# Attention and a mixture of experts on one core: transposes and similarities ahead of down products, one-hots by VectorE only

## The reference

```python
def xattn(h, adj_raw, Wq, Wk, gamma_raw):      # h = ctx, adj_raw = layernorm(x)
    Q = (h @ Wq.T) in 4 heads; K = (h @ Wk.T) in 4 heads
    sim = einsum('bhnd,bhmd->bnm', Q, K) / (sqrt(32) * 4)
    threshold = top_k(sim, 153)[..., -1:]       # a row's 153rd largest
    A = sigmoid(sim) * (sim >= threshold)
    A = (A + swapaxes(A, -1, -2)) * 0.5
    return (1 - gamma) * adj_raw + gamma * A    # gamma = sigmoid(gamma_raw)
x = x + xattn(ctx, layernorm(x), ...)
h = layernorm(x)                                # 2048 rows
scores = sigmoid(h @ router_w)                  # 32 experts in 8 groups of 4
# biased scores: best 4 groups (by their top 2), of them the best 8 experts of a row
w = scores of the 8 / their sum * 2.5
routed = sum over the 8 of w * (silu(h @ w_gate[e]) * (h @ w_up[e])) @ w_down[e]   # inner size 256
shared = (silu(h @ sw_gate) * (h @ sw_up)) @ sw_down                               # inner size 512
x = x + routed + shared
```

## Time and profile before

| what | us |
|---|---|
| median of three runs (1103.67 to 1105.88) | 1104.59 |
| the profiled execution, whole time | 1106.17 |
| its span, from first to last instruction | 1104.4 |
| stage 0, up to the bound of stage 1 | 93.5 |
| stages 1, 2 | 77.9, 78.3 |
| stage 3, to the end of the first block | 72.5 |
| from there to the expert tiles at full pace (375) | 52.8 |
| expert tiles | 729 |
| TensorE, VectorE, ScalarE, POOL busy | 921.8, 573.0, 487.4, 481.6 |

### The profile page before, as it was taken

The page is one execution under the profiler, slowest core; times in us unless marked ns, Lnnn a source line. Parts: engine busy times, 40 slices in busy tenths (PEclk is TensorE's granted clock), DMA queues, the critical chain, the costliest instruction groups (busy, mean ns, idle before and its releaser), DMA issues.

```text
span 1104.4 us, 21250 instructions
## 1 busy us (share of the span) xinstructions
PE 921.8 (83%) x4604; PEld 490.0 (44%) x4605; DVE 573.0 (52%) x1288; ACT 487.4 (44%) x993; POOL 481.6 (44%) x380
## 2 busy tenths in 40 slices
PE   3367676675787799999999999999999999999985
PEld 1143242342544455554545555545544454545542
DVE  5947686675785444445544444454454545454321
ACT  5284453462213344445444444454454545454331
POOL 2021051051343245555455456555456453655543
PEclk8568887886888899999999999999999999999998
DMA  5111021010123867677977777777878788786654
GB/s 178 59 39 50 1 77 50 30 51 1 73 70 116 255 147 162 141 171 165 259 178 159 170 174 170 166 170 173 211 157 196 211 183 237 159 183 112 122 107 71
DMA packets 90267, 149.25 MB, mean 135 GB/s; under 512 B 9648, under 2 KB 46768, under 8 KB 90224
## 3 DMA queue, kind: packets, MB, share of 16 engines
q0 software_dynamic: 33120, 80.64, 37.3%
q1 hardware_dynamic: 57104, 68.13, 18.7%
HBM read 101.55 MB, written 47.20 MB: 135 GB/s over the span
## 4 chain that ended last, share of the span: by engine, by line
PE 45%; issue 8%; DVE 4%; ACT 4%; DVEq 3%; DMA 3%; ACTq 2%; SPq 1%; POOL 0%; POOLq 0%
PE bank L256 37%; PE bank L1488 4%; DMA stage_dn<-in_L_ffn_w_down_dram 3%; PE bank L1479 3%; ACT gu L238 3%; DVEq L1159 2%; ACTq L1159 2%; DVE gu L245 1%; DVE hid L1395 1%; DVE dn L248 1%; DVE mark_p L393 1%; DVE hT L1404 0%; ACT silu L1255 0%; ACTq L238 0%; PE bank L1459 0%
## 5 line engine op out<-in xcount | busy, mean ns | idle before, releaser
L256 PE MATMUL bank<-gu,xgT 128*128 x1764 | 407.8, 381 | 12.2 <-issue 8.2
L1205 POOL DMA_INDIRECT out_dram<-y,ids_i x145 | 240.9, 1661 | 287.3 <-DMA out_dram<-y,ids_i 158.0
L256 PEld LDWEIGHTS bank<-gu,xgT 128*128 128x128 f16 x1764 | 172.9, 98 | 193.5 <-issue 22.6
L256 PE MATMUL bank<-dn,hT 128*128 x870 | 212.1, 380 | 16.7 <-issue 16.6
L1193 POOL DMA_INDIRECT xg<-xrows,ids_i x153 | 157.6, 1030 | 64.0 <-issue 41.1
L1395 DVE SCALAR_TENSOR_TENSOR hid<-bank,xg,silu 128x256 f32<-128x256 f32 x146 | 70.4, 482 | 207.7 <-ACT silu L1255 207.7
L1267 ACT CAST hT<-bank 128x256 f16<-128x256 f32 x146 | 53.7, 368 | 225.7 <-PE bank L1479 225.7
L1274 ACT ACTIVATE y<-bank 128x512 f32<-128x512 f32 x145 | 86.6, 597 | 134.4 <-PE bank L256 134.4
L1404 DVE TENSOR_TENSOR hT<-bank,hT 128x256 f16<-128x256 f32 x146 | 61.8, 423 | 151.3 <-ACT hT L1267 151.3
L256 PEld LDWEIGHTS bank<-dn,hT 128*128 128x128 f16 x870 | 84.9, 98 | 91.9 <-issue 24.8
L256 PE MATMUL bank<-xT,gu 128*128 128x512 f16 x384 | 97.3, 417 | 16.0 <-DVE hid L307 16.0
(11 more groups left out here) (217 smaller groups left out, 820.7 us busy)
## 6 DMA issues: line engine op xcount, KB each, us to landing
stage_gu<-in_L_ffn_w_gate_dram SPq DMA_DIRECT2D x32, 512.0 KB
stage_gu<-in_L_ffn_w_up_dram SPq DMA_DIRECT2D x32, 512.0 KB
stage_dn<-in_L_ffn_w_down_dram SPq DMA_DIRECT2D x32, 512.0 KB
x_sb<-in_x_dram SPq DMA_DIRECT2D x4, 1024.0 KB, 6.5
xrows<-adj SPq DMA_DIRECT2D x4, 1024.0 KB, 4.2
out_dram<-acc SPq DMA_DIRECT2D x4, 1024.0 KB, 5.4
xg<-xrows,ids_i POOLq DMA_INDIRECT x153, 4.4
out_dram<-y,ids_i POOLq DMA_INDIRECT x145, 5.1
```

Source lines behind the costliest of these rows:

```text
L256: last = nc.tensor.matmul(out_ap, stationary(a, c), moving(w, c), start=(c == 0 and (a, w) == parts[0]), stop=(c == chunks - 1 and (a, w) ...
L1205: g_.indirect_dma_start(out, bass.IndirectOffsetOnAxis(ap=ids_i[:, t:t + 1], axis=0), y[:, t % YS, :], None, compute_op=ALU.add).then_inc( ...
```

## The change

On TensorE, `adjacency_T`, `rank_tokens` and `similarities` of a stage go ahead of all down products; these are together behind them (three ahead of `rows_T`, the fourth behind `logits`). `sum_marks` is run a stage later, ahead of the context transposes, with its sum in another bank (`MARKB`); `turn_found` moves behind gate and up piece 3. On ScalarE the copies move with them. On VectorE the order of the shared expert's instructions changes: `s_product` 0 of a batch goes to the end of its own stage, the `s_add`s come later (the fourth behind `routing`), and search step 1 comes ahead of the one-hots. POOL's `part_parts` is gone: VectorE compares for `mark_q` itself and multiplies in a second instruction; the groups of one-hots are spread, two ahead of `routing` and two behind it (in stage 3 all four ahead). `count_columns` moves from the second block to the end of the first, and `count_tiles` to the front of VectorE's list in the second. The core of the diff:

```diff
+        IDS, INFO = 2, 3
         DB = (7, 5, 6, 7)
         FEW, RANKS = slice(P, P + RT), slice(2 * P, 4 * P)
         RANKB = (MISC,) * (B - 1) + (SIMB[0],)
+        MARKB = (SIMB[1],) * (B - 1) + (TB[0],)
...
         def sum_marks(pe, b):
-            pe.wait_ge(S["xhi_ready"], RT * min(b + 2, B))
+            if b + 2 < B:
+                pe.wait_ge(S["sim_copied"], RT * (b + 3))
+            else:
+                pe.wait_ge(S["adjT_used"], RT * B)
+                pe.wait_ge(S["xhi_ready"], RT * B)
             for g in range(RT):
                 pe.wait_ge(S["marks_p_ready"], RT * b + g + 1)
                 pe.wait_ge(S["marks_q_ready"], RT * b + g + 1)
                 for k in range(TOP_EXPERTS):
-                    t = nc.tensor.matmul(bank[TB[0]][:, g * 2 * E:(g + 1) * 2 * E], mark_p[:, g, k, :], mark_q[:, g, k, :],
+                    t = nc.tensor.matmul(bank[MARKB[b]][:, g * 2 * E:(g + 1) * 2 * E], mark_p[:, g, k, :], mark_q[:, g, k, :],
                                          start=(k == 0), stop=(k == TOP_EXPERTS - 1))
...
                 pe.wait_ge(S["scores_ready"], b + 2)
+                pe.wait_ge(S["ranks_used"], b + 1)
...
-        def part_parts(pool, b, g):
-            if b:
-                pool.wait_ge(S["marks_summed"], b)
-            nc.gpsimd.tensor_tensor(mark_q[:, g, :, :], upto[:, 0:2 * E].unsqueeze(1).to_broadcast([P, TOP_EXPERTS, 2 * E]),
-                                    part_of[:, g, :].unsqueeze(2).to_broadcast([P, TOP_EXPERTS, 2 * E]), ALU.subtract).then_inc(S["parts_apart"], 1)
-
         def mark_parts(dve, b, g):
             n = RT * b + g
-            dve.wait_ge(S["parts_apart"], n + 1)
-            nc.vector.tensor_scalar(mark_q[:, g, :, :], mark_q[:, g, :, :], 0.0, row_idf[:, n:n + 1], ALU.is_equal, ALU.mult).then_inc(S["marks_q_ready"], 1)
+            if b:
+                dve.wait_ge(S["marks_summed"], b)
+            nc.vector.tensor_tensor(mark_q[:, g, :, :], upto[:, 0:2 * E].unsqueeze(1).to_broadcast([P, TOP_EXPERTS, 2 * E]),
+                                    part_of[:, g, :].unsqueeze(2).to_broadcast([P, TOP_EXPERTS, 2 * E]), ALU.is_equal).then_inc(S["parts_found"], 1)
+            dve.wait_ge(S["parts_found"], n + 1)
+            nc.vector.tensor_scalar(mark_q[:, g, :, :], mark_q[:, g, :, :], row_idf[:, n:n + 1], None, ALU.mult).then_inc(S["marks_q_ready"], 1)
+
+        def mark(dve, b, g):
+            mark_slots(dve, b, g)
+            mark_parts(dve, b, g)
...
-                    if b >= 3:
-                        pe.wait_ge(S["found_ready"], b - 2)
...
                     pe.wait_ge(S["adj_ready"], RT * b + RT)
+                    if b >= 2:
+                        pe.wait_ge(S["found_ready"], b - 1)
...
                         s_gate_up(pe, p, 2)
                     if p >= 1:
-                        turn_found(pe, p - 1)
+                        sum_marks(pe, p - 1)
                     if b + 1 < B:
                         context_T(b + 1)
                     if p >= 0:
                         s_gate_up(pe, p, 3)
+                    if p >= 1:
+                        turn_found(pe, p - 1)
                     if b + 1 < B:
                         mixed(b + 1)
@@ -665,29 +679,26 @@
                     if p >= 1:
                         pe.wait_ge(S["tab_ready"], p)
                     nc.tensor.matmul(bank[MISC][0:1, FEW], ones[:, 0:1], few[:, :], start=True, stop=True).then_inc(S["few_summed"], 1)
-                    if p >= 0:
-                        s_down(pe, p, 0)
                     adjacency_T(b)
                     if p >= 0:
                         rank_tokens(pe, p)
                     if b + 1 < B:
                         similarities(b + 1)
                     if p >= 0:
-                        s_down(pe, p, 1)
-                        s_down(pe, p, 2)
+                        for i in range(RT - 1):
+                            s_down(pe, p, i)
                     rows_T(b)
+                    logits(b)
                     if p >= 0:
-                        s_down(pe, p, 3)
-                    logits(b)
+                        s_down(pe, p, RT - 1)
                     s_gate_up(pe, b, 0)
                     if b + 1 < B:
                         s_gate_up(pe, b, 1)
-                        if p >= 0:
-                            sum_marks(pe, p)
                     else:
                         sum_marks(pe, p)
                         s_gate_up(pe, b, 1, (0,))
                         rank_tokens(pe, b)
+                        count_columns()
                         s_gate_up(pe, b, 1, (1,))
                         turn_found(pe, p)
...
                     if p >= 1:
-                        copy_table(act, p - 1)
+                        copy_found(act, p - 1)
                     if more:
                         context_mixed(b + 1)
                     if p >= 0:
                         s_high(act, p, 2)
                         s_silu(act, p, 3)
+                    if p >= 1:
+                        copy_table(act, p - 1)
...
-                        s_product(dve, p, 0)
+                        s_product(dve, p, 1)
                         dve.wait_ge(S["xlo_ready"], RT * b)
                         dve.wait_ge(S["scores_ready"], b)
                     ch.settle()
                     for i in range(RT):
                         ch.done(v.scalar_tensor_tensor(under[:, i, :], junk[:, i, :], LOWEST, sim[:, i, :], ALU.mult, ALU.add))
+                    ch.settle()
+                    for i in range(RT):
+                        ch.done(v.max(top8[:, i, :], under[:, i, :]))
                     if p >= 0:
-                        s_product(dve, p, 1)
-                    ch.settle()
-                    for i in range(RT):
-                        ch.done(v.max(top8[:, i, :], under[:, i, :]))
+                        s_product(dve, p, 2)
                     ch.step(v.tensor_scalar(rank[:, :], cnt[:, :], -1.0, float(KEEP), ALU.mult, ALU.add))
                     ch.step(v.tensor_tensor(at_rank[:, :, :], one_to_8[:, :].unsqueeze(1).to_broadcast([P, RT, 8]),
                                             rank[:, :].unsqueeze(2).to_broadcast([P, RT, 8]), ALU.is_equal))
                     v.tensor_reduce(few[:, :], at_rank[:, :, :], AX.X, ALU.add).then_inc(S["few_ready"], 1)
                     ch.step(v.tensor_tensor(top8[:, :, :], top8[:, :, :], at_rank[:, :, :], ALU.mult))
                     ch.step(v.tensor_reduce(lo[:, :], top8[:, :, :], AX.X, ALU.add))
-                    if p >= 0:
-                        s_product(dve, p, 2)
                     if b + 1 < B:
                         x_stats(b + 1, range(0, RT // 2))
...
-                    if p >= 0:
-                        s_add(dve, p, 0)
...
                     if p >= 0:
-                        s_add(dve, p, 1)
+                        s_add(dve, p, 0)
...
-                    if b == 1:
-                        dve.wait_ge(S["rows_stored"], 16)
-                        dve.wait_ge(S["zeroed"], 16)
                     bound(b)
                     if b == 0:
                         convert_low(dve, 0)
@@ -1088,24 +1092,29 @@
                         search_step(b + 1, 0)
                         coefficients(b + 1)
                     if p >= 0:
-                        s_add(dve, p, 2)
+                        s_add(dve, p, 1)
                         find_keys(dve, ch, p)
-                        s_add(dve, p, 3)
-                        for g in range(RT):
-                            mark_slots(dve, p, g)
-                        if not more:
-                            for g in range(RT):
-                                mark_parts(dve, p, g)
                     if more:
                         search_step(b + 1, 1)
+                    if p >= 0:
+                        s_add(dve, p, 2)
+                        for g in range(2 if more else RT):
+                            mark(dve, p, g)
                     routing(b)
+                    if p >= 0:
+                        s_add(dve, p, 3)
                     if more:
                         search_step(b + 1, 3)
                         if p >= 0:
-                            for g in range(RT):
-                                mark_parts(dve, p, g)
+                            mark(dve, p, 2)
                         else:
                             convert_low(dve, 1)
+                        if b == 0:
+                            dve.wait_ge(S["rows_stored"], 16)
+                            dve.wait_ge(S["zeroed"], 16)
+                        s_product(dve, b, 0)
+                        if p >= 0:
+                            mark(dve, p, 3)
                         search_step(b + 1, 4)
                     else:
                         s_product(dve, b, 0)
...
-                mark_slots(dve, b, 0)
-                mark_slots(dve, b, 1)
+                count_tiles()
+                mark(dve, b, 0)
+                mark(dve, b, 1)
```

(25 more changed lines are left out.)

13 lines of the change are left out of this document (1 added, 12 removed).

## The result

The changed kernel takes 1068.67 us (median of 4 runs, 1066.09 to 1070.42), the kernel before 1105.24 beside it (4 runs, 1103.67 to 1106.62). The ratio is 0.9668, with a 95% interval of 0.9639 to 0.9697. That is 36.6 us saved where 32 was predicted. The profiled execution takes 1070.4 us with a span of 1068.6, so 35.8 us of span are to be accounted for.

The account below looks back on a forecast made before the run. The prediction took a chain of waits between TensorE and VectorE, neither full, to set the attention stages. Savings of 25.3 + 4.2 + 2.4 = 31.9 us took the profiled 1106.17 to 1074.3, the median to 1073, range 1063 to 1087.

Parts of the forecast that it names:

- A to A: From the end of adj in one stage to that in the next: 68.5 us where it was 78.
- Adjacency first: From the end of adj to `xn`: transposes start at once, squares come 5.0 us sooner (bounds 4 to 6).
- rival (a): Down products 0 to 2 stay at 1.2 GHz, 15 us not 10.3, delaying `xn`'s transposes: 1088, chance 0.12.
- Search step 1 first: VectorE before routing: step ends at 221.1, scores come at 224.3, one-hots fill the wait.
- One-hots by VectorE only: A group costs 2.1 us alone, the first two 6.2 together beside POOL; routing at 227.9 instead of 237.7.
- (b): Rival: one-hots cost 3.4 us a group, with 12 of 16 groups on the path: 1088, chance 0.12.
- (d): Rival, slower: every compare and multiplication at its dearest row, 5.5 us a group: 1118, chance 0.03.
- `s_product` 0 in its own stage: First half of stage 1: it fills an idle before step 4, gate/up 2 starts at 92.8 not 97.0; 6.1 saved.
- The first 24 products cost 8.2 us: TensorE after `s_add` 3: gate/up 1 starts after an idle, next two sets 5.3 each, `few` at 258.3.
- Rival (c): The wait for bank 7 keeps TensorE cold until `few`: +12 us in two stages, 1097, chance 0.03.
- rival (e): Nothing comes of it, because the expert part waits for weights, not its start: 1104.6, chance 0.02.
- The rule on the shared port: Alone it doubles all compares meeting POOL's work, the later instruction blocking; by the rows only each stage's first two groups.

Follow-up runs that it names:

- The filler around the rows: The changed kernel with useless TensorE products around the row transposes of stages 1 and 2: 1072.16 us, beside 1069.24 for the changed kernel.
- the undone kernel above: The changed kernel with POOL subtracting for `mark_q` again, VectorE comparing with zero and multiplying in one instruction: 1073.19 us, ratio 0.971.
- Adjacency first alone: The kernel before with only adjacency transposes, ranks and similarities ahead of down products and each `s_add` one place later: 1084.56 us, ratio 0.9815.

## Why the prediction was right, and where it was off

The mechanism is the one predicted, and 36.6 us were saved for 32. By the spans, term by term: first half of stage 1 6.7 (predicted 6.1), stage 1 to 2 14.0 (9.7), stage 2 to 3 13.0 (9.5), stage 3 3.7 (4.2), dispatch 1.3 (2.4), expert part -2.9 (0). The sum is 35.8.

That the total came so near is in part luck. The first block gave 7.9 us more than forecast: its end is at 284.8, where I had put 292 to 294, and A to A is 64.1 us for 68 to 69. The dispatch and the expert part gave 4.0 less, and the 2.9 of the expert part are within what one execution differs by from the next. TensorE's idle before gate/up 1, 6 to 8 us by the forecast, was 1.9 in stages 1 and 2: of the signs named, these three failed.

**Adjacency first: right.** The transposes were taken with under 1 us of waiting. Squares came 7.4 and 7.8 us behind in stages 1 and 2 (7.2 predicted), `xn` at A + 19.0 and 19.4 (19.0). The down products are no obstacle: 36 in 7.93 us at the full clock, so rival (a), which gave them 15, falls.

**Search step 1 first: right.** find_keys ended at A + 26.8 (26.7 predicted), and routing was entered at A + 32.9 (34.0); in stage 2 at 27.1 and 33.3. Undone, it cost 11.8 us.

**One-hots by VectorE only: right, and somewhat cheaper.** The 512-wide compare took 0.68 us (0.6 estimated), a group 2.4, two ahead of routing 4.7 where I had put 6.2 for meeting POOL's base. POOL's base took 6.20 and 6.24 us instead of 5.04, so most of the contention fell upon POOL. Beside POOL's low halves in the dispatch the compare did take 1.65 us, twice. Rivals (b) and (d) fall: no group took 3 us in the stages. From A to S it was 41.6 and 42.0 us (42.7 predicted).

**`s_product` 0 in its own stage: as forecast, but not isolated.** Gate/up 2 of stage 1 started at 92.3 (92.8 predicted), and the wait of 4.84 us before it is gone in the stages after. No experiment undoes this part alone, so its share of the saving isn't shown.

**The step that was mis-sized is TensorE from `s_add` 3 to the next adj: "The first 24 products cost 8.2 us".** S to A took 22.5 us, 25.8 predicted; this is 3.3 of the 4.4 that the period was shorter (22.1 in stage 2). I had TensorE finish gate/up 0 at 229.2 in the old times, 7.4 us ahead of S, by giving the logits 3.65 us, read from a kernel in which down product 3 stands right ahead of them, and down product 3 half of what two take at the full clock. In the new order three short sets of row transposes with waits between them stand there, the granted clock is 0.50, the logits take 6.87 and down product 3 4.01. That was not on the path, for gate/up 1 waits for `s_add` 3 anyway, and the scores were still there 1.8 us before VectorE took them. With S itself 1.1 us earlier it ate the idle, 1.9 us were left, and TensorE went on at the full clock: 48 products in 10.52 us. The filler around the rows turned this back: idle 6.84 and 5.16 us, 12.65 and 13.36 us for the products. So the new wait for bank 7 was foreseen, its length was not. Rival (c), the cold clock up to `few`, falls with it. Even behind 6.84 us of idle the 48 products lost only 2.1 us, and 2.8 behind 5.16. One sum of mine is off too: 19 us of VectorE's work from S at 236.6 end at 255.6, not at 254.3. Nothing hung on it, for `few` came later, and VectorE still waits 1.1 us for `few`.

**Stage 3: right.** There the idle is 7.37 us, 12 products take 4.05 (5.0 predicted), the ranks stand behind them, and VectorE waits 4.1 us for the ranks. **Dispatch: 1.3 for 2.4,** within the bounds given; the two compares of 1.65 us make VectorE's list 1.9 longer there. **Expert part:** I called it 730 us from 375 on; it kept its length within what it varies by and began 38.7 us earlier, so rival (e) falls.

**The rule on the shared port.** The Trainium skill, SBUF — State Buffer, "Who interferes with whom", says that a VectorE instruction with two SBUF inputs contends with a GpSimd one that reads SBUF. The trace agrees that one of the two waits; what I had wrong is which. The first two groups of stages 1 and 2 ran beside POOL's base at 1.21 and 0.68 us, as groups 3 and 4 did without it (1.22 and 0.68), and only the multiplication took 0.59 to 0.67 for 0.35. Of the base's four instructions in stage 1, the two that ran ahead of the compares took 0.78 and 0.77 us, the two beside them 2.33 and 2.37. My row of 5.04 for the base held one such wait already: 2.79 us and three times 0.76. In the dispatch, where POOL's low half had started 1.0 and 0.3 us before the compare, VectorE waited (1.65 us for 0.68, twice), as it did beside POOL's subtraction in the undone kernel above.

The parts don't add up: undone one by one they cost 11.6, 11.8 and 4.5 us, 27.9 of 36.6. Much of the rest is in a part that none of the three undoes: A of stage 1 stays at 108.8 to 109.7 in all of them, where it was 115.8, so the 6 to 7 us of its first half are kept. Adjacency first alone brings 20.8 and its undoing costs 11.6; the warm transposes and the shorter idle of the undone kernel are a part of the difference, the whole isn't shown.

## What to carry to other kernels

When work is reordered, take the duration of each TensorE set from its new predecessor, not from its old row: here the same logits took 3.65 us behind products and 6.87 behind short transposes with waits (3.66 where the waits were shorter). Then ask whether the set is on the path; a slow set in front of a wait costs nothing, and can keep the engine warm for what comes behind it, while speeding it up made the first block's end 4.9 us later. Look at the engine that is next in line before an idle is closed: two of the idles closed here moved the limit to VectorE or to a cold start elsewhere.

## What the runs showed of the hardware

- Behind row transposes with idles of 1.89, 1.86 and 0.32 us the granted clock was 0.50 (133.0 to 139.7 us); in stage 3, with idles of 1.93, 0.73 and 0.33 us, it was still 1.00 for the logits (254.7 to 258.2) and 0.60 behind them (258.2 to 262.5). Behind an idle of 1.93 us that followed 24 products in 5.34 us, it stayed at 1.00 (150.8 to 161.2). The length of the last idle alone doesn't tell the clock behind it.
- Instructions of 4 elements a partition on VectorE took 0.16 us alone, 0.21 and 0.42 beside POOL's base, and 0.96 and 0.97 beside its two-input subtraction; a 1024-wide compare 1.21 without POOL's subtraction and 1.53 beside it.
- Two executions of one kernel differ by 5.6 us in the 740 us of the expert part alone. A single profile can't settle a term of 3 us there.
